# GpSimd's wait for a place in the ring of gathered rows: VectorE's add in place of TensorE's sum

## The chip, the cores and the metric

The kernel runs on one core of a Trainium2 chip. The metric is the device time of one execution in microseconds (us); the kernel before takes 2083.07 us, the median of 3 runs. Engines are named as in the profile: PE is TensorE's matmuls, PEld its weight loads, DVE VectorE, ACT ScalarE, POOL GpSimd, SP SyncE.

## What is computed

A network of four layers over 3125 nodes with 256 features and 50000 edges, all in float32. Layers one and three are graph layers, layers two and four mixtures of experts. The change touches only the sums over edges in the two graph layers. Cut to that, the reference is

```python
# layer 1: edges carry 64 features, dst is sorted
sender_features = nodes[senders]
msg_in = jnp.concatenate([sender_features, edges], axis=-1)
messages = msg_in @ W_message
agg = jax.ops.segment_sum(messages, receivers, num_segments=total_nodes)
...
# layer 3: h_sparse keeps the 32 largest of each row of feat @ W_neigh
msg = h_sparse[src]
summed = jax.ops.segment_sum(msg, dst, num_segments=n)
neigh = summed / jnp.maximum(deg, 1.0)[:, None]
return h_self + neigh
```

The kernel sums the gathered rows first and multiplies the sums by the weights afterwards.

## The kernel before

The nodes are 25 tiles of 128 rows. The edges, sorted by target, are cut into 98 groups of 512 (`NG` = 98), each of four columns of 128 edges (`GC` = 4). A group's targets lie within a window of 128 nodes. `sums_and_nodes` is called twice, with the tag O0 for layer 1 (rows from `n_rows`, with edge features) and with O1 for layer 3 (rows from `sparse_rows`, without). It runs the class `Sums` for the groups, last group first, and beside it the work on each node tile as soon as its sums are complete: `NodeMlp` in O0, a layer norm, three matrix layers and another norm; `NeighbourMeans` in O1, much shorter.

One group, number `o` in the order of work, passes through four engines:

- GpSimd, `gather`: four indirect DMAs (line 743), each of which fetches 128 rows of 1 KB, by the edges' source numbers, into place `o % 8` of the ring `G` (`GR` = 8 places). From the ninth group on it first waits for a place (the line that the change touches, 741).
- VectorE, `hot` (line 767): the one-hot matrix `OH` of the group's targets, in a ring of four.
- TensorE, `products` (line 758): the sum. It multiplies rows by `OH` into one of two PSUM banks: 8 matrix products of 128x128 in O1 (16 records in the profile), 12 in O0 (24 records), where 4 of them read the edge features `EA`. It waits for `OH`, the gathered rows and VectorE's add of group `o - 2`, which frees the bank, and its last product increments `summed`.
- VectorE, `add` (line 779): after writing the `OH` of group `o + 2` it waits for `summed`, adds the bank to the window of the table `sumT`, and increments `added`.

TensorE and VectorE take the groups at fixed points among their other work on node tiles (`group(0)` to `group(3)` in the methods `pe` and `dve`), 3 or 4 groups in each step; each engine runs its list in order, so an add stands behind whatever VectorE has before it. GpSimd does nothing else in these two stretches than the 392 indirect DMAs, in order. The edge features come by SyncE's DMAs, which wait for the sum of group `o - 4` and are not touched. ScalarE's copy of finished sums waits for `added`. The stages before, between and after (normalising, routing, experts, the product with both weight matrices) are separated by barriers of all engines, so a stretch that ends later moves everything behind it.

Of the kernel before, what the change touches and what calls it, by code (L numbers as in the profile page):

```python
# [19 lines left out]
GR = 8  # L20
# [6 lines left out]
def build(nc, a, out):  # L27
# [52 lines left out]
    with ExitStack() as ctx:  # L80
# [632 lines left out]
        class Sums:  # L713
# [24 lines left out]
            def gather(self, pool, o):  # L738
                g, s = NG - 1 - o, o % GR
                if o >= GR:  # L740
                    pool.wait_ge(self.summed, o + 1 - GR)
                for k in range(GC):
                    pool.indirect_dma_start(out=self.G[:, s, k, :], out_offset=None, in_=self.rows_dram,  # L743
                                            in_offset=bass.IndirectOffsetOnAxis(ap=src_tab[:, g, k:k + 1], axis=0)
                                            ).then_inc(self.gathered[s], 16)
# [1166 lines left out]
```

## Time and profile before

| what | value |
|---|---|
| median of 3 runs | 2083.07 us (2081.49 to 2083.76) |
| the profiled execution | 2088.08 us, its span 2086.3 us |
| PE busy | 1273.2 us (61%) |
| DVE busy | 758.2 us (36%) |
| ACT busy | 388.7 us (19%) |
| POOL busy | 1094.5 us (52%) |
| O0, from the first gather to the last | from 56.2 to 667.6 us |
| O1, from the first gather to the last | from 1234.5 to 1801.2 us |

The page gives each engine's busy time over the whole span, and the costliest groups of instructions with the idle time ahead of them and who ended it. The two lines on `L743 POOL DMA_INDIRECT` stand at its head: 392 gathers of 985 ns in O0 and 392 of 961 ns in O1. An idle time that is put down to "issue" is one in which the profile saw nothing waited for; "remote" is a wait that ended on a semaphore whose increment the profile can't give to an instruction that ended just then. TensorE's records carry a measured start and a modelled end.

### The profile page before, as it was taken

The page shows a single profiled execution, that of the slowest core. Times are in us where ns is not written, and L with a number is a line of the kernel's source. Part 1 is how long each engine was busy: PE and PEld are TensorE (multiplying, and loading weights), DVE is VectorE, ACT ScalarE, POOL GpSimd, SP SyncE. Part 2 cuts the span into 40 slices and gives each one's busy share as a digit, 9 for nine tenths or more (in the row PEclk, how much of TensorE's full clock was granted, in tenths as well). Part 3 has the DMA queues.
Part 4 walks back from the last instruction along what each step waited for, and adds up shares of the span by engine and source line. Part 5 has one row for each costly group of instructions (what it writes and reads, how often), then busy time and mean ns, then how long its engine had stood idle before and what let it go on. Part 6 is the DMA issues. An engine that isn't in the chain of part 4 may idle for free. (4 is left out here: it accounts for less than half of the span.)

```text
span 2086.3 us, 29303 instructions
## 1 busy us (share of the span) xinstructions
PE 1273.2 (61%) x7947; PEld 1132.2 (54%) x7948; DVE 758.2 (36%) x2256; ACT 388.7 (19%) x1296; POOL 1094.5 (52%) x1166
## 2 busy tenths in 40 slices
PE   0267877777788727999936533446454554539920
PEld 0256777767677626999812213445454544528920
DVE  5022444444444451111159951222222222364433
ACT  0000111111111102444334410000000000005533
POOL 2656656556665003222187736666666666315455
PEclk9778888889898759999956656677666766769965
DMA  5334434434433008999822233333333333203445
GB/s 175 103 101 113 111 102 109 108 102 115 109 107 106 18 5 302 351 353 348 294 78 81 78 125 95 91 94 100 98 97 98 99 96 99 62 32 107 130 127 156
DMA packets 204046, 264.53 MB, mean 127 GB/s; under 512 B 75150, under 2 KB 155040, under 8 KB 203670
## 3 DMA queue, kind: packets, MB, share of 16 engines
q0 software_dynamic: 48192, 131.35, 22.2%
q1 hardware_dynamic: 152882, 129.47, 18.9%
q10 hardware_dynamic: 2852, 2.24, 0.4%
q8 instruction: 58, 0.95, 0.2%
q14 instruction: 62, 0.51, 0.1%
HBM read 231.24 MB, written 32.04 MB: 126 GB/s over the span
## 5 line engine op out<-in xcount | busy, mean ns | idle before, releaser
L743 POOL DMA_INDIRECT O0G<-n_rows,src_tab x392 | 386.0, 985 | 267.0 <-issue 144.7
L743 POOL DMA_INDIRECT O1G<-sparse_rows,src_tab x392 | 376.8, 961 | 200.6 <-issue 121.3
L758 PE MATMUL O1ps_sums<-O1OH,O1G 128*128 128x128 f32 x1568 | 262.2, 338 | 158.9 <-DVE sumT L779 80.1
L758 PEld LDWEIGHTS O1ps_sums<-O1OH,O1G 128*128 128x128 f32 x1568 | 249.2, 250 | 166.8 <-issue 166.6
L758 PE MATMUL O0ps_sums<-O0OH,O0G 128*128 128x128 f32 x1568 | 227.2, 298 | 63.4 <-issue 49.7
L758 PEld LDWEIGHTS O0ps_sums<-O0OH,O0G 128*128 128x128 f32 x1568 | 212.3, 212 | 71.3 <-issue 71.0
L779 DVE TENSOR_TENSOR sumT<-sumT,O1ps_sums 128x256 f32 x98 | 41.2, 421 | 441.4 <-remote 340.4
L779 DVE TENSOR_TENSOR sumT<-sumT,O0ps_sums 128x384 f32 x98 | 54.3, 554 | 334.2 <-remote 191.9
L1363 POOL DMA_INDIRECT e0xs<-token_rows,e0idx x64 | 60.5, 945 | 204.7 <-ACT e0idx L1432 202.9
L758 PE MATMUL O0ps_sums<-O0OH,O0EA 128*128 128x128 f32 x784 | 115.9, 289 | 21.6 <-issue 21.2
L1389 PE MATMUL e0ps_h<-e0xT,e0W 128*128 128x128 f32 x1024 | 126.1, 277 | 1.5 <-DMA e0W<-in_L_ffn_w 1.5
L1644 PE MATMUL m0ps_d<-w_dense,m0nT 128*128 128x512 f32 x100 | 85.7, 1008 | 61.9 <-ACT m0nT L1617 61.9
L1389 PEld LDWEIGHTS e0ps_h<-e0xT,e0W 128*128 128x128 f32 x1024 | 120.7, 194 | 1.8 <-DMA e0W<-in_L_ffn_w 1.7
L1403 PE MATMUL e0ps_y<-e0W,e0hidT 128*128 128x256 f32 x512 | 120.9, 379 | 0.0
L758 PEld LDWEIGHTS O0ps_sums<-O0OH,O0EA 128*128 128x128 f32 x784 | 105.3, 205 | 21.2 <-issue 20.9
L1484 DVE TENSOR_TENSOR e0ys<-e0ps_y,e0b_rows 128x256 f32<-128x256 f32 x64 | 27.2, 425 | 226.2 <-PE e0ps_y L1403 226.2
L1763 PE MATMUL O1ps_g<-gate_w,O1nT 128*128 128x8 f32 x100 | 22.7, 337 | 141.8 <-ACT O1nT L1742 118.3
L962 PE MATMUL O0ps<-O0hT,w_mlp 128*128 128x128 f32 x600 | 96.8, 309 | 18.1 <-issue 10.5
L1363 POOL DMA_INDIRECT e1xs<-token_rows,e1idx x56 | 55.5, 992 | 91.4 <-ACT e1idx L1432 56.5
L1763 PEld LDWEIGHTS O1ps_g<-gate_w,O1nT 128*128 128x128 f32 x100 | 20.8, 291 | 149.0 <-ACT O1nT L1742 124.9
L962 PEld LDWEIGHTS O0ps<-O0hT,w_mlp 128*128 128x128 f32 x600 | 89.0, 224 | 20.1 <-issue 11.1
L1403 PEld LDWEIGHTS e0ps_y<-e0W,e0hidT 128*128 128x128 f32 x512 | 92.5, 190 | 9.9
(298 smaller groups left out, 2012.6 us busy)
## 6 DMA issues: line engine op xcount, KB each, us to landing
e0W<-in_L_ffn_w SPq DMA_DIRECT2D x128, 512.0 KB
O0EA<-in_edge_attr SPq DMA_DIRECT2D x97, 128.0 KB
expert_out<-e0ys SPq DMA_DIRECT2D x64, 128.0 KB
expert_out<-e1ys SPq DMA_DIRECT2D x56, 128.0 KB
O0G<-n_rows,src_tab POOLq DMA_INDIRECT x392
O1G<-sparse_rows,src_tab POOLq DMA_INDIRECT x392
e1W_all<-in_L_ffn_w SPq DMA_DIRECT2D x16, 256.0 KB
n_rows<-NR SPq DMA_DIRECT2D x5, 640.0 KB
```

Source lines behind the costliest of these rows:

```text
L743: pool.indirect_dma_start(out=self.G[:, s, k, :], out_offset=None, in_=self.rows_dram, in_offset=bass.IndirectOffsetOnAxis(ap=src_tab[:, g ...
L758: last = nc.tensor.matmul(self.ps[o % 2][:, half * P:(half + 1) * P], rows, self.OH[:, h, k, :], start=(k == 0), stop=(k == GC - 1))
L779: nc.vector.tensor_tensor(window, window, self.ps[o % 2][:, 0:self.halves * P].rearrange("p (h w) -> p h w", h=self.halves), ALU.add).then ...
L962: last = nc.tensor.matmul(ps_l[:, m * P:(m + 1) * P], w_mlp[:, l, k, m * P:(m + 1) * P], hT[:, s, k, :], start=(k == 0), stop=(k == K2 - 1))
L1363: pool.indirect_dma_start(out=xs[:, s, :], out_offset=None, in_=token_dram, in_offset=bass.IndirectOffsetOnAxis(ap=idx[:, s:s + 1], axis=0 ...
L1389: last = nc.tensor.matmul(ps_h[:, s % 2, j * P:(j + 1) * P], W1[:, s, k, j * P:(j + 1) * P], xT[:, s, k, :], start=(k == 0), stop=(k == K2 ...
L1403: last = nc.tensor.matmul(ps_y[:, s % 2, 0:D], hidT[:, s, j, :], rows, start=(j == 0), stop=(j == FJ - 1))
L1484: nc.vector.tensor_tensor(ys[:, s, :], ps_y[:, s % 2, 0:D], tile_of(b2_rows, e), ALU.add).then_inc(y_ready, 1)
L1644: last = nc.tensor.matmul(ps_d[:], nT[:, s, k, :], w_dense[:, k, :], start=(k == 0), stop=(k == K2 - 1))
L1763: last = nc.tensor.matmul(self.ps_g[:, 0:E1], self.nT[:, k, :], gate_w1[:, k, :], start=(k == 0), stop=(k == K2 - 1))
```

## The change

GpSimd's wait for a free place in the ring is moved from TensorE's semaphore to VectorE's. Both count groups, and the count waited for stays the same. One line changes; it is used in both stretches, 90 times in each. No instruction is added or removed.

```diff
             def gather(self, pool, o):
                 g, s = NG - 1 - o, o % GR
                 if o >= GR:
-                    pool.wait_ge(self.summed, o + 1 - GR)
+                    pool.wait_ge(self.added, o + 1 - GR)
                 for k in range(GC):
                     pool.indirect_dma_start(out=self.G[:, s, k, :], out_offset=None, in_=self.rows_dram,
```

## Rows read from the trace of the kernel before

**Rows 1.** Windows: both stretches while GpSimd gathers, and O1's end after it.

```profile
core 0: us, PE busy (x) PEld busy (x) DVE busy (x) ACT busy (x) POOL busy (x), PEclk, DMA share, GB/s
56.00:668.00 612.00, 443.76 (x3069) 415.98 (x3069) 231.49 (x651) 78.04 (x241) 386.02 (x392) 0.84 0.40 109
...
1234.00:1802.00 568.00, 276.22 (x1662) 264.32 (x1662) 125.25 (x323) 21.64 (x67) 376.83 (x392) 0.69 0.36 103
1802.00:1815.00 13.00, 10.75 (x92) 10.32 (x92) 5.22 (x13) 1.49 (x4) 0.00 (x0) 1.00 0.06 20
```

**Rows 2.** Waits of POOL: us in total, times, longest us.

```profile
POOL O0G L743 <- remote: 79.3, 39, 6.5
POOL O1G L743 <- remote: 71.7, 27, 6.1
...
POOL O0G L743 <- PE O0ps_sums L758: 43.0, 14, 4.1
...
POOL O1G L743 <- PE O1ps_sums L758: 7.6, 6, 2.5
```

**Rows 3.** Timeline of POOL, O1: start us, us; in brackets idle before, releaser.

```profile
1558.04 0.94 POOL L743 DMA_INDIRECT O1G<-sparse_rows,src_tab  x1 [2.34 <-remote]
...
1575.43 0.94 POOL L743 DMA_INDIRECT O1G<-sparse_rows,src_tab  x1 [2.72 <-remote]
...
1589.34 0.95 POOL L743 DMA_INDIRECT O1G<-sparse_rows,src_tab  x1 [0.30 <-issue]
1592.90 0.94 POOL L743 DMA_INDIRECT O1G<-sparse_rows,src_tab  x1 [2.61 <-remote]
```

**Rows 4.** Timeline of DVE, the adds of the same stretch.

```profile
1563.21 0.42 DVE L779 TENSOR_TENSOR sumT<-sumT,O1ps_sums 128x256 f32 x1 [3.19 <-issue]
...
1581.35 0.42 DVE L779 TENSOR_TENSOR sumT<-sumT,O1ps_sums 128x256 f32 x1 [3.38 <-PE O1ps_sums L758]
...
1592.77 0.42 DVE L779 TENSOR_TENSOR sumT<-sumT,O1ps_sums 128x256 f32 x1 [9.73 <-remote]
```

**Rows 5.** Timeline of POOL, two restarts in O0.

```profile
285.11 1.03 POOL L743 DMA_INDIRECT O0G<-n_rows,src_tab  x1 [2.17 <-remote]
...
293.65 0.94 POOL L743 DMA_INDIRECT O0G<-n_rows,src_tab  x1 [3.74 <-PE O0ps_sums L758]
```

**Rows 6.** Timeline of DVE, the adds at these restarts.

```profile
286.50 0.55 DVE L779 TENSOR_TENSOR sumT<-sumT,O0ps_sums 128x384 f32 x1
...
293.52 0.56 DVE L779 TENSOR_TENSOR sumT<-sumT,O0ps_sums 128x384 f32 x1 [5.87 <-PE O0ps_sums L758]
```

**Rows 7.** Waits of PE: the only one on O0's gathered rows.

```profile
PE O0ps_sums L758 <- DMA O0G<-n_rows,src_tab: 12.6, 1, 12.6
```

**Rows 8.** Timeline of PE, O0, while GpSimd fills the ring.

```profile
73.93 1.13 PE L758 MATMUL O0ps_sums<-O0OH,O0G 128*128 128x128 f32 x8 [2.12 <-issue]
...
87.10 0.37 PE L758 MATMUL O0ps_sums<-O0OH,O0G 128*128 128x128 f32 x1 [2.43 <-issue]
```

**Rows 9.** Timeline of POOL, the first pause of each stretch.

```profile
108.41 0.94 POOL L743 DMA_INDIRECT O0G<-n_rows,src_tab  x1 [6.49 <-remote]
...
1285.58 0.94 POOL L743 DMA_INDIRECT O1G<-sparse_rows,src_tab  x1 [6.09 <-remote]
```

**Rows 10.** Timeline of PE, O1: the first two sums, and sums about the restarts.

```profile
1246.88 6.72 PE L758 MATMUL O1ps_sums<-O1OH,O1G 128*128 128x128 f32 x32 [24.62 <-issue]
...
1559.67 1.64 PE L758 MATMUL O1ps_sums<-O1OH,O1G 128*128 128x128 f32 x11
...
1580.53 2.02 PE L758 MATMUL O1ps_sums<-O1OH,O1G 128*128 128x128 f32 x16
```

**Rows 11.** Timeline of DVE, O1: the second add, and the first and last of the last five.

```profile
1285.45 0.42 DVE L779 TENSOR_TENSOR sumT<-sumT,O1ps_sums 128x256 f32 x1 [28.47 <-remote]
...
1805.41 0.42 DVE L779 TENSOR_TENSOR sumT<-sumT,O1ps_sums 128x256 f32 x1 [1.79 <-PE O1ps_sums L758]
...
1813.22 0.42 DVE L779 TENSOR_TENSOR sumT<-sumT,O1ps_sums 128x256 f32 x1 [1.81 <-PE O1ps_sums L758]
```

## The prediction

> **What bounds the kernel now.** I read the windows first. The gathers of O0 and O1 take 612 and 568 us, 57% of the span, and in neither is an engine busy throughout: of O0's 612 us PE has 444 and POOL 386, of O1's 568 us PE has 276 and POOL 377 [rows 1]. Next the timeline of POOL: a gather is 0.95 us with 0.30 us to the next [rows 3], so a group of four takes 5.0 us and 98 groups 490 us. What O0 and O1 last beyond 490 us, GpSimd stands still. The table of waits says on what: in O0 53 pauses with 122.3 us (79.3 + 43.0, 39 + 14), in O1 33 with 79.3 us (71.7 + 7.6, 27 + 6) [rows 2]. These contain each the usual 0.30 us. They are the waits of line 741: the ring is full, and GpSimd goes on 0.13 us after an add begins (1575.43, 1592.90 against 1592.77; 293.65 against 293.52) [rows 3 to 6], because both wait for the same sum. TensorE in turn hardly waits for rows: the table has one such wait in O0, 12.6 us at its start [rows 7].
>
> So GpSimd waits for TensorE, TensorE not for GpSimd's rows, and one would call TensorE the bound. The rows don't bear that out in O1. Its last five adds, after the last gather, begin 7.81 us from first to last, 1.95 us a group [rows 11]; while gathers run a group takes 568/98 = 5.8 us. TensorE is slow only beside GpSimd. The start of the stretches shows it directly. In O0, PE does 8 products in 1.13 us from 73.93 us on, and then one in 2.8 us (0.37 and 2.43 idle, put down to nothing) [rows 8]; that ends when GpSimd has filled the ring and paused for 6.49 us [rows 9]. In O1 the products of the first two groups are on record from 1246.88 to 1253.60 [rows 10], yet the second add begins at 1285.45 with VectorE idle for 28.47 us before it [rows 11], 6 us after GpSimd's first run of gathers ended (1285.58 less 6.09) [rows 9]. In the middle of O1: GpSimd restarts at 1575.43; a sum arrives at 1581.35, 5.9 us later; the next one's products are on record from 1580.53 to 1582.55 [rows 10], but its add begins at 1592.77 [rows 4], 2.5 us after GpSimd paused again at 1590.29 [rows 3]. I conclude that in a run of gathers sums get through for some 6 us, then they are held until about 2 us after the next pause. What holds them (the products, their write to PSUM or the semaphore) the profile doesn't say; it shows only the moments.
>
> **The change.** One edit, one answer to work out: when GpSimd goes on, and what that costs. No instruction is added, and queued behind the wait are only the four gathers of the group and all later ones; the edge features' DMAs are in SyncE's queue and keep their own wait.
>
> The delay of one restart. Now GpSimd starts 0.13 us after the add's start, then 0.13 us after its end, as far as another semaphore takes as long. In O1 an add is 0.42 us [rows 4]: 33 x 0.42 = 14 us. In O0 it is 0.55 us, but VectorE may be at other work. At 285.11 GpSimd goes on with the sum, and the add begins at 286.50 [rows 5, 6]: the restart would move to 286.50 + 0.55 + 0.13 = 287.18, by 2.07 us. Nine of the 53 pauses look so, the others like the one at 293.65, by 0.56 us: 44 x 0.55 + 9 x 2.1 = 43 us, 0.81 us each. Waits that don't stop GpSimd now may stop it for a few tenths; I leave them at nothing, the add of eight groups back is long done there. Delays in sum: 57 us.
>
> What reaches the end. If rows were what TensorE waits for, or GpSimd the bound, all 57 us; if TensorE were the bound on its own, none. Neither fits what I read. In the pattern above a pause costs l, in which GpSimd does nothing, and buys a window w after the restart, in which sums get through. The sums of a stretch need a fixed total of such windows. A later restart adds e to both: TensorE works on in e. So the number of pauses falls by w/(w + e), each costs l + e, and all pauses together change by (l + e)/l x w/(w + e). From the rows l is 79.3/33 = 2.40 us in O1 and 122.3/53 = 2.31 us in O0, and e is 0.42 and 0.81 us. For w the upper end is 6 us (the sum at 5.9 us came in time, the next did not). The lower end is 3 us: after the restart at 1558.04 products that end on record at 1561.31 [rows 10] have their add at 1563.21 [rows 4], 1.9 us later instead of 0.1, so lateness has set in some 3 us after the restart.
> - w = 6: O1 1.175 x 0.935 = 1.098, +7.8 us; O0 1.351 x 0.881 = 1.190, +23.2 us; sum +31 us.
> - w = 3: O1 1.175 x 0.877 = 1.031, +2.4 us; O0 1.351 x 0.787 = 1.064, +7.8 us; sum +10 us.
> I take the middle, w = 4.5: O1 +5.9 us, O0 +17.7 us, sum +23.6 us, since either end is one pair of rows. Nothing behind gives it back, because a barrier follows each stretch. The profiled execution, 2088.1 us (its span 2086.3), would take about 2112 us; against the median it is 2083.1 + 23.6 = 2106.7, and I forecast 2106 us. A difference of 4 us (0.2%) is about what a measurement can tell from none.
>
> **Rivals.**
>
> First, the ring hides it (2083 us, 2080 to 2087). When GpSimd waits, up to eight groups are gathered ahead of TensorE, and 7 groups of 5.8 us are 40 us of stock against a delay of at most 2.1 us. For it: only one wait for rows in O0 [rows 7]. If TensorE's slowness had a cause of its own, the restart's moment wouldn't matter. Against it: the last adds at 1.95 us and the two starts, where the hold ends with GpSimd's pause [rows 8 to 11]. The Trainium skill speaks for this rival: its page "SBUF — State Buffer", section "SBUF: two separate sides", says that only the ports which GpSimd and VectorE share cause contention, and that TensorE never waits on anyone. By that rule the sum would be nothing. The trace doesn't agree as I read it, with one product in 2.8 us beside gathers. The page "DMA: Bandwidth & Descriptors", section "Anatomy of one DMA", gives some 2.0 us fixed and 436 GB/s, from which I estimate 2.3 us for a gather of 128 KB; by that too rows would lie ready long before use.
>
> Second, the whole delay (2125 to 2140 us). GpSimd does nothing useful in its pauses, so 490 us plus pauses is the length, and if TensorE can use none of the longer pause, because its next product stands behind VectorE's or ScalarE's work on tiles, all 57 us come: 2140. For it: PE's own waits for ScalarE in O1 are of that kind. Against: in O0 PE is busy 73% of the time [rows 1], so it has work queued.
>
> Third, faster (2060 to 2079 us). O0 has 90 groups that wait and 53 pauses, 1.7 groups a run, so some 35 runs of two. A run of two groups is 10 us, and sums are held from about 6 us after the restart to 12 us, 2 us after the pause began; a run of one group is 5 us and holds nothing. If the wait for adds, which come less evenly than sums, splits runs of two, TensorE wins each time up to those 6 us; I take half, 3 us, as products begun go on meanwhile. Then 8 runs split would cancel the 23.6 us, and 14 would give 2065 us. It decides where two adds follow each other by more than 5.0 us. For it: adds like the one at 286.50 are 1.5 us later than their sum. Against it: such an add pushes the wait for itself and not that for the next, so as many runs should be joined as split.
>
> **How the numbers follow.** Forecast, part of the delay arrives (2090 to 2125 us): 0.60. The ring hides it: 0.17. The whole delay: 0.06. Faster: 0.17. That the wait doesn't do as it says I leave out: the same count on a semaphore that lags by one add can't let GpSimd go earlier. Within 0.2% fall the hidden case, 0.02 of the faster and 0.01 of the forecast's lower edge: same 0.20, slower 0.65, faster 0.15. For 8 in 10 the range goes from 2076 us (which leaves out 0.13, most of the faster case) to 2128 us (which holds w = 6 at 2114 us and twice its distance from the forecast, and leaves out 0.07, the whole delay and a little).
>
> **What would show it.** In the profile of the changed kernel every restart of GpSimd after a pause should come 0.13 us after the end of an add, not its start. Pauses should be fewer or as many, and longer: in O1 about 33 with 85 us, in O0 about 50 with 140 us. PE's busy time should stay. O0 should be longer by about 18 us from first gather to last add and O1 by 6 us, and all other stages as long as before. The forecast is wrong in its core if the pauses' total grows by under 4 us (the ring hides it) or falls (the third rival), and in its size if PE's holds begin at another time after a restart than before.

## The result, and the profile after

The change makes the kernel slower: 2111.05 us, the median of 4 runs (2104.76 to 2115.39), against 2083.41 us for the kernel before (4 runs, 2081.49 to 2086.55). The ratio is 1.0121, with a 95% interval of 1.0099 to 1.0143. The forecast was 2106 us.

The profiled execution of after took 2115.39 us, its span 2113.5 us, 27.2 us more than the span of before. Where they are is seen from the line of all gathers and the line of all adds (in each: shortest, median and longest ns, then the start of the first and of the last). Before, by line 743 and by the tile `sumT`:

```profile
L743 POOL DMA_INDIRECT O0G<-n_rows,src_tab x392: 940/946/2028, 56.2 to 666.7; - x196
L743 POOL DMA_INDIRECT O1G<-sparse_rows,src_tab x392: 940/946/1467, 1234.5 to 1800.3; - x196
```

```profile
L779 DVE TENSOR_TENSOR sumT<-sumT,O0ps_sums x98: 541/555/558, 72.3 to 694.5; 128x384 f32 x98
L779 DVE TENSOR_TENSOR sumT<-sumT,O1ps_sums x98: 414/422/424, 1256.0 to 1813.2; 128x256 f32 x98
```

After:

```profile
L743 POOL DMA_INDIRECT O0G<-n_rows,src_tab x392: 943/949/2028, 57.0 to 692.3; - x196
L743 POOL DMA_INDIRECT O1G<-sparse_rows,src_tab x392: 943/949/1386, 1251.4 to 1821.1; - x196
```

```profile
L779 DVE TENSOR_TENSOR sumT<-sumT,O0ps_sums x98: 539/555/558, 72.4 to 714.1; 128x384 f32 x98
L779 DVE TENSOR_TENSOR sumT<-sumT,O1ps_sums x98: 414/422/424, 1272.8 to 1840.5; 128x256 f32 x98
```

From the first gather to the last add O0 goes from 638.3 to 657.1 us (+18.8) and O1 from 578.7 to 589.1 us (+10.4). That is 29.2 us, and all other stages together are 2 us shorter, as the prediction had it. In O0 the gathers themselves take longer, 635.3 us for 610.5 (+24.8), and the rest after the last gather is 6.0 us shorter (21.8 for 27.8). In O1 it is the other way: the gathers take 569.7 for 565.8 us (+3.9), and the rest after them 19.4 for 12.9 us (+6.5). These splits compare one execution with one other. Executions of the changed kernel on a single chip differ by up to 19 us (the third chip, below), so a few us in a part of a stretch carry little.

The waits of GpSimd in the trace after (us in total, times, longest us), which answer to [rows 2]:

```profile
POOL O0G L743 <- DVE sumT L779: 146.3, 57, 6.7
...
POOL O1G L743 <- DVE sumT L779: 78.3, 25, 6.4
```

O0 has 57 waits with 146.3 us for 53 with 122.3, O1 has 25 with 78.3 for 33 with 79.3. So O0 has more and longer pauses (2.57 us for 2.31 each), O1 fewer and longer ones (3.13 for 2.40) with nearly the same sum. Together they grew by 23.0 us. The prediction had said that it would be wrong in its core if they grew by under 4 us. Counted instead as idle times over 0.4 us in the timeline of POOL, whatever the profile puts them down to, O0 goes from 51 with 121.5 us to 61 with 151.9, and O1 from 31 with 80.2 to 22 with 79.9; the expectations of some experiments use this count.

A restart in O1 of after, in the timeline of POOL, and the add that released it in that of DVE (start us, us; in brackets idle before, releaser):

```profile
1332.10 1.15 POOL L743 DMA_INDIRECT O1G<-sparse_rows,src_tab  x1 [4.19 <-DVE sumT L779]
```

```profile
1331.41 0.42 DVE L779 TENSOR_TENSOR sumT<-sumT,O1ps_sums 128x256 f32 x1 [15.88 <-remote]
```

The add ends at 1331.83 and GpSimd goes on at 1332.10, 0.27 us later. Before, it went on 0.13 us after an add's start [rows 3, 4]. In O1 a restart is thus 0.56 us later against the same add (0.42 + 0.27 - 0.13), where the prediction had 0.42. All 83 restarts after an idle time over 0.4 us in this trace (61 in O0, 22 in O1) come 0.26 to 0.28 us after the end of an add. Counted in the same way over the trace of before, restarts moved to 0.27 us after the end of their adds would be 0.97 us later on average in O0 and 0.56 in O1, 49 and 17 us in sum. In O0, the same two timelines of after:

```profile
293.19 1.15 POOL L743 DMA_INDIRECT O0G<-n_rows,src_tab  x1 [4.39 <-DVE sumT L779]
...
301.13 0.95 POOL L743 DMA_INDIRECT O0G<-n_rows,src_tab  x1 [3.02 <-DVE sumT L779]
...
306.39 0.95 POOL L743 DMA_INDIRECT O0G<-n_rows,src_tab  x1 [0.55 <-DVE sumT L779]
```

```profile
300.30 0.56 DVE L779 TENSOR_TENSOR sumT<-sumT,O0ps_sums 128x384 f32 x1 [6.78 <-PE O0ps_sums L758]
...
305.56 0.56 DVE L779 TENSOR_TENSOR sumT<-sumT,O0ps_sums 128x384 f32 x1 [2.09 <-PE O0ps_sums L758]
```

Here too it is 0.27 us (300.86 to 301.13, 306.12 to 306.39). The last row is something that before doesn't have: a group that would have followed without a pause waits 0.55 us instead of the usual 0.30, because adds 5.26 us apart are wider apart than the 5.0 us of a group. Counting the groups between idle times over 0.4 us in the timeline of POOL, O0 has 16 runs of one group and 32 of two before, and 39 of one and 17 of two after. Idle times under 1.1 us are 13 after and none before, those over 2.6 us 29 after and 13 before.

PE's busy time, which the prediction expected to stay, is 1286.2 us for 1273.2, 1% more.

### The profile page after: what moved, and what is told of

It is laid out like the page before. It is cut to its first block and busy times, and to the rows that moved or that the text cites. A ratio compares the mean times of both kernels' runs of the same rounds, so it can differ in the third digit from the quotient of the medians.

```text
span 2113.5 us, 29303 instructions
## 1 busy us (share of the span) xinstructions
PE 1286.2 (61%) x7947; PEld 1136.9 (54%) x7948; DVE 759.7 (36%) x2256; ACT 388.8 (18%) x1296; POOL 1094.2 (52%) x1166
## 5 line engine op out<-in xcount | busy, mean ns | idle before, releaser
L758 PEld LDWEIGHTS O0ps_sums<-O0OH,O0G 128*128 128x128 f32 x1568 | 216.6, 217 | 54.4 <-issue 54.0
L1363 POOL DMA_INDIRECT e0xs<-token_rows,e0idx x64 | 60.7, 948 | 204.6 <-ACT e0idx L1432 202.8
L962 PE MATMUL O0ps<-O0hT,w_mlp 128*128 128x128 f32 x600 | 99.9, 311 | 25.7 <-issue 18.8
L1484 DVE TENSOR_TENSOR e0ys<-e0ps_y,e0b_rows 128x256 f32<-128x256 f32 x64 | 27.2, 425 | 226.3 <-PE e0ps_y L1403 226.3
L1446 ACT ACTIVATE e0hidT<-e0ps_h,b_cols 128x128 f32<-128x128 f32 x256 | 73.3, 368 | 92.4 <-issue 53.3
L923 ACT ACTIVATE O0yT<-O0ps,b_mlp 128x128 f32<-128x128 f32 x100 | 31.3, 364 | 305.3 <-remote 222.8
```

The costliest lines, as they stand in the source:

```text
L758: last = nc.tensor.matmul(self.ps[o % 2][:, half * P:(half + 1) * P], rows, self.OH[:, h, k, :], start=(k == 0), stop=(k == GC - 1))
L923: last = nc.scalar.activation(yT[:, m, :], ps_l[:, m * P:(m + 1) * P], ACT.Relu, bias=b_mlp[:, l, m:m + 1])
L962: last = nc.tensor.matmul(ps_l[:, m * P:(m + 1) * P], w_mlp[:, l, k, m * P:(m + 1) * P], hT[:, s, k, :], start=(k == 0), stop=(k == K2 - 1))
L1363: pool.indirect_dma_start(out=xs[:, s, :], out_offset=None, in_=token_dram, in_offset=bass.IndirectOffsetOnAxis(ap=idx[:, s:s + 1], axis=0 ...
L1446: last = nc.scalar.activation(hidT[:, s, j, :], ps_h[:, s % 2, j * P:(j + 1) * P], func, bias=b1_cols[:, ds(e * FJ + j, 1)])
L1484: nc.vector.tensor_tensor(ys[:, s, :], ps_y[:, s % 2, 0:D], tile_of(b2_rows, e), ALU.add).then_inc(y_ready, 1)
```

## The experiments

They ran on four other chips, here called the second to the fifth, each beside runs of the kernel before on the same chip. That turned out to matter more than any edit. The kernel before takes 2083 us on the first chip, 1879 on the second, 2068 on the third, 2063 on the fourth and 1877 on the fifth. Every comparison below is within one chip.

### Second chip: the wait in O0 alone, a ring of five, a pause for every group

```diff
-                    pool.wait_ge(self.summed, o + 1 - GR)
+                    pool.wait_ge(self.added if self.with_edges else self.summed, o + 1 - GR)
```

> GpSimd waits for VectorE's add in O0 alone; in O1 it waits for the sum as before. Theory H (sums are held while GpSimd gathers without a pause, so that part of each restart's delay arrives): O0 takes 18 us more from first gather to last add, O1 as before, in all 2101 us (2094 to 2108). Rival W (a restart's whole delay arrives in O0, the 43 us worked out for it, and something in O1 gives 15 us back): 2126 us. Rival E (equal shares, the cost goes by waits and not by an add's length or lateness): 2097 us.

Measured: 1878.73 us (10 runs) against 1878.95 us (19 runs), ratio 0.9996, 0.9982 to 1.0010. All three forecasts in it start from 2083 us, and the base itself is 204 us lower here. The costliest groups of this run's trace (busy us, mean ns | idle before, by releaser) say why:

```profile
L743 POOL DMA_INDIRECT O0G<-n_rows,src_tab x392 | 385.1, 982 | 162.1 <-issue 159.7 <-DVE sumT L779 2.4
L743 POOL DMA_INDIRECT O1G<-sparse_rows,src_tab x392 | 380.0, 969 | 133.1 <-issue 129.1 <-PE O1ps_sums L758 4.0
...
L779 DVE TENSOR_TENSOR sumT<-sumT,O0ps_sums 128x384 f32 x98 | 54.3, 554 | 242.2 <-PE O0ps_sums L758 242.2
L779 DVE TENSOR_TENSOR sumT<-sumT,O1ps_sums 128x256 f32 x98 | 41.4, 422 | 371.4 <-PE O1ps_sums L758 371.4
```

GpSimd never pauses for a place: its wait for the add has 2.4 us in all, in 8 waits of the usual 0.30 us, and the 392 gathers of a phase follow each other in 504 us (O0) and 499 us (O1). VectorE's adds wait only until a product of TensorE ends. None of the adds' waits is "remote", where before on the first chip has 191.9 and 340.4 us of these. Such waits, with adds up to 32 us after the last record of their products (1253.60 and 1285.45) [rows 10, 11], are what I called held sums, and this chip has none. The 204 us between the chips are about the 201.6 us of pauses in [rows 2] (122.3 + 79.3). So on this chip the ring is never full, and where GpSimd's wait never ends last, the change's half in O0 costs nothing. In O0 it is TensorE that waits for rows here, 92.3 us in all, where it had 12.6 us on the first chip [rows 7]:

```profile
L758 PE MATMUL O1ps_sums<-O1OH,O1G 128*128 128x128 f32 x1568 | 278.1, 351 | 215.2 <-issue 138.7 <-DVE O1OH L767 47.8 <-DMA O1G<-sparse_rows,src_tab 28.7
...
L758 PE MATMUL O0ps_sums<-O0OH,O0G 128*128 128x128 f32 x1568 | 210.3, 291 | 97.6 <-DMA O0G<-n_rows,src_tab 92.3 <-DVE O0OH L767 3.4 <-DVE sumT L779 1.4
```

The same rows speak against an obvious rival, that TensorE merely calculates faster on this chip. Its products of gathered rows take 351 ns on average in O1 and 291 ns in O0; on the first chip they take 338 and 298 ns. In O1 they are slower here and still no sum is late.

```diff
-                if o >= GR:
-                    pool.wait_ge(self.summed, o + 1 - GR)
+                if o >= 5:
+                    pool.wait_ge(self.summed, o + 1 - 5)
```

> GpSimd waits for TensorE's sum as before, but uses the ring as if it had 5 places: each restart waits for the sum three groups later, some 17 us. Theory H: TensorE still has five groups of stock, the number of windows it needs is the same, so the stretches take as long as before; the first run of gathers is 6 groups long in place of 9, and the long hold that follows it shorter, so 2066 to 2085 us. Rival W (each later restart moves what follows by its delay): the change delayed a restart by 0.4 to 0.8 us and cost 27.6 us; a delay of 17 us, even if only the 86 first ones of it count once, gives over 2180 us. Rival B (TensorE is bound by itself, and the ring hides GpSimd): 2083 us, with the first hold as long as before.

Measured: 1876.49 us (10 runs) against 1878.95, ratio 0.9988, 0.9972 to 1.0005, for the same reason. Neither of these two runs tells the theories apart; they show only that five places are enough where no sum is late.

```diff
+                pool.wait_ge(self.idled, o) if o else None
+                nc.gpsimd.memset(self.idle[:], 0.0).then_inc(self.idled, 1)
```

These lines stand at the end of `gather`, with a tile `idle` of 128x1024.

> As before, and after each group of four gathers GpSimd sets 1024 columns of a scratch tile to zero (some 0.95 us), and waits for the one before: a group takes it some 6.3 us and no run of gathers is longer than 5 us. Theory H: no run is long enough to hold sums, if a gap of over 1 us ends a run. The pauses for a place in the ring nearly go (under 10 in each stretch after the first), an add follows its last product by 0.1 to 0.2 us, and the stretches last 98 x 6.3 = 617 us and a tail: O0 some 15 us shorter, O1 some 40 us longer, in all 2095 to 2120 us. Rival B (TensorE's slowness is its own): adds come late by 5 to 11 us in O1 as before, and the ring pauses stay, 10 us less in sum than the 1.25 us a group that GpSimd takes longer.

Measured: 2033.73 us (1 run), 155 us more. In the timeline of POOL the memset is 0.96 us, and a group takes 5.83 us (1356.49 to 1362.32) instead of 5.0:

```profile
1356.49 0.95 POOL L745 DMA_INDIRECT O1G<-sparse_rows,src_tab  x1 [0.17 <-issue]
...
1361.19 0.96 POOL L749 MEMSET O1idle<- 128x1024 f32 x1
1362.32 0.95 POOL L745 DMA_INDIRECT O1G<-sparse_rows,src_tab  x1 [0.17 <-issue]
```

196 groups x 0.83 us are 163 us, nearly all of which arrive (155). On such a chip GpSimd's own gathers set the length of both phases, and nearly each us that they are delayed is a us of the kernel's time. There were no held sums on which the pause could have worked, so the question that this run was made for is not answered by it, and the edit was not timed on a chip with pauses.

### Third chip: the changed kernel again, and two places with either wait

The changed kernel itself, timed again:

> The changed kernel itself, timed against the kernel before on whatever chip this call gets. What is at stake: on the second chip the kernel before takes 1879 us instead of 2083, and GpSimd's 392 gathers of each phase run without a single pause (added in O0 alone, and a ring of 5, both gave 1879 +- 3 there). Theory 'pauses': the move only costs where GpSimd waits for a place at all; if the kernel before takes about 1879 us here, the changed one is within 0.2% of it (1875 to 1883), its trace without pauses; if the kernel before takes about 2083 us here, the changed one takes 2105 to 2117. Rival 'own price': the wait for VectorE's add costs something by itself in each of 196 groups, whatever the chip: over 0.4% slower (1887 us or more) on the faster chip too.

Measured: 2093.65 us (6 runs) against 2068.03 us (11 runs), ratio 1.0116, 1.0084 to 1.0147. The chip is one with pauses, and the ratio is that of the first chip within the error. O0 has 47 waits with 125.3 us for the add, O1 24 with 68.0. From the first gather to the last add O0 takes 642.0 us and O1 584.6. The kernel before has no trace on this chip; on the fourth, where it is 5 us faster, these are 616.9 and 576.0 us (below).

```diff
-                if o >= GR:
-                    pool.wait_ge(self.summed, o + 1 - GR)
+                if o >= 2:
+                    pool.wait_ge(self.summed, o + 1 - 2)
```

> GpSimd waits for TensorE's sum of the group two before, so the ring of 8 is used as 2 places; all else as before. Worked out from the traces of the second chip: from a group's first gather to the end of its last 4.7 us, rows there 1.8 us later, the sum 2.9 us in O0 (0.25 us after the rows) and 2.0 to 3.8 us in O1, 0.1 us to the restart. So two groups in turn take 9.7 us in O0 and 8.6 to 10.4 us in O1, against the 10.0 us that GpSimd needs for them. Theory 'plain chain' (no sums that come late): +0 to +15 us over the kernel before. Theory 'hold' (sums come late while GpSimd gathers, as in the first chip's traces, and are let go about 2 us after it pauses): 12 to 12.5 us for two groups, 590 to 610 us for each phase, so 2090 to 2150 us on a chip where the kernel before takes 2083. What a late sum costs with no place to spare is in this run.

Measured: 2048.81 us (4 runs), ratio 0.9897, 0.9866 to 0.9927, so 19 us faster than before. Neither theory had a gain: "hold" had 7 to 67 us more than before, so it is wrong by 26 us or more, and "plain chain" has its sign wrong.

The next has the same edit with `self.added` for `self.summed`:

> As the run with two places, but GpSimd waits for VectorE's add of the group two before: the change on record made where each wait ends last. The add ends 0.70 us (O0, 384 columns) and 0.56 us (O1, 256 columns) after the sum in the second chip's traces. Theory 'whole' (each restart later by all of the add): against the run with two places +0.35 us a group in O0 and +0.28 in O1, less what GpSimd's own 5.0 us a group hide of it (0.15 in O0, nothing to 0.28 in O1): +20 us in O0 and +15 to +25 in O1, +35 to +45 us in all. Theory 'hold' with its release by the pause: the later restart lets more sums through, +15 to +30 us. Rival 'hidden': the add's time is made up elsewhere, under +10 us.

Measured: 2101.75 us (4 runs), ratio to before 1.0153, 1.0122 to 1.0184, and 52.9 us over the run with two places and the wait for the sum. That is above all three ranges. The lines of the gathers and of the adds with the wait for the sum (a fence for each view):

```profile
L743 POOL DMA_INDIRECT O0G<-n_rows,src_tab x392: 940/946/2034, 57.5 to 657.6; - x196
L743 POOL DMA_INDIRECT O1G<-sparse_rows,src_tab x392: 940/946/1453, 1205.1 to 1773.4; - x196
```

```profile
L779 DVE TENSOR_TENSOR sumT<-sumT,O0ps_sums x98: 542/554/557, 70.7 to 665.2; 128x384 f32 x98
L779 DVE TENSOR_TENSOR sumT<-sumT,O1ps_sums x98: 420/422/424, 1222.5 to 1780.1; 128x256 f32 x98
```

and with the wait for the add:

```profile
L743 POOL DMA_INDIRECT O0G<-n_rows,src_tab x392: 940/947/2034, 56.5 to 700.6; - x196
L743 POOL DMA_INDIRECT O1G<-sparse_rows,src_tab x392: 940/947/1422, 1244.8 to 1822.6; - x196
```

```profile
L779 DVE TENSOR_TENSOR sumT<-sumT,O0ps_sums x98: 541/555/557, 69.5 to 706.8; 128x384 f32 x98
L779 DVE TENSOR_TENSOR sumT<-sumT,O1ps_sums x98: 420/422/424, 1261.2 to 1829.3; 128x256 f32 x98
```

The gathers of O0 go from 600.1 to 644.1 us (+44.0), those of O1 from 568.3 to 577.8 us (+9.5). The delay weighs 4.6 times as much in O0 as in O1; with eight places the gathers have +24.8 against +3.9. No give-back is seen in O0 with two places. In the run with the wait for the sum, 60 restarts follow an idle time over 0.4 us, and if each came 0.27 us after the end of its add they would be 43 us later in sum: 44.0 arrive. In O1 there are 60 too, with 33 us in sum, and 9.5 arrive.

### Fourth chip: O1 alone, three places, the kernel before, and O1 without GpSimd

The kernel before, unedited, for its trace on this chip:

> The kernel before, unedited, for its trace on the same chip as the others of this call. If it takes over 2060 us here: GpSimd's pauses 110 to 130 us in O0 and 72 to 85 us in O1, with adds up to 20 us behind the products. If it takes about 1879 us: no pause, every add 0.14 us after the last product of its group but for some in O0.

Measured: 2065.13 us in this one run; the median of before on this chip is 2063.45 us (15 runs). Its gathers and adds:

```profile
L743 POOL DMA_INDIRECT O0G<-n_rows,src_tab x392: 940/946/2027, 57.7 to 649.4; - x196
L743 POOL DMA_INDIRECT O1G<-sparse_rows,src_tab x392: 940/946/1442, 1213.0 to 1772.0; - x196
```

```profile
L779 DVE TENSOR_TENSOR sumT<-sumT,O0ps_sums x98: 539/554/557, 74.4 to 674.6; 128x384 f32 x98
L779 DVE TENSOR_TENSOR sumT<-sumT,O1ps_sums x98: 410/421/424, 1234.2 to 1789.0; 128x256 f32 x98
```

Its pauses are 102.5 us in O0 (51) and 67.3 us in O1 (29), somewhat fewer than expected: the faster a chip runs this kernel, the fewer us of pauses its trace has (201.6 at 2083 us, 169.8 at 2063 us, none in the runs on the chip with 1879 us).

```diff
-                    pool.wait_ge(self.summed, o + 1 - GR)
+                    pool.wait_ge(self.summed if self.with_edges else self.added, o + 1 - GR)
```

> GpSimd waits for VectorE's add in O1 alone; O0 is as before. On a chip whose traces have GpSimd's pauses (the kernel before over 2060 us): the forecast had +5.9 us for O1 of +23.6; the two traces of the first chip have +10.4 us from the first gather of O1 to its last add, with the pauses' sum unchanged (80.2 and 79.9 us, 31 and 22 of them). So +4 to +11 us here, ratio 1.002 to 1.005, and pauses of 76 to 84 us in O1. Rival 'half': each phase bears half of the change's 25 us (+12 us or more, 1.006 and over). Rival 'all in O0': within 0.1%. On a chip without pauses (the kernel before about 1879 us): no difference.

Measured: 2076.51 us (10 runs) against 2063.45, ratio 1.0058, 1.0031 to 1.0084. The median says +13 us, the interval +6 to +17, so it takes in much of what I expected and the rival "half"; only "all in O0" is out. The profiled execution was one of the shortest of its kernel (span 2062.3 us), and its O1 takes 579.0 us from the first gather to the last add (rows below), 3.0 us more than the 576.0 us of the unedited kernel: the gathers are 8.8 us longer (567.8 for 559.0) and the rest after them 5.8 us shorter (11.2 for 17.0). How much of the change's 1.2% is O1's stays open between these.

```profile
L743 POOL DMA_INDIRECT O1G<-sparse_rows,src_tab x392: 940/946/1496, 1213.7 to 1781.5; - x196
```

```profile
L779 DVE TENSOR_TENSOR sumT<-sumT,O1ps_sums x98: 412/421/424, 1233.6 to 1792.7; 128x256 f32 x98
```

```diff
-                if o >= GR:
-                    pool.wait_ge(self.summed, o + 1 - GR)
+                if o >= 3:
+                    pool.wait_ge(self.summed, o + 1 - 3)
```

> GpSimd waits for TensorE's sum of the group three before; all else as before. With two places the pauses' sum was 203 us (112.9 in O0, 90.1 in O1) against 202 us (121.7 and 80.2) with eight in the first chip's trace, and what was gained was the end: the last add of O0 came 7.3 us after the last gather instead of 27.5. Theory 'rate' (TensorE's sums get through only so many per us beside gathers, and the places only say when GpSimd learns of it): three places give 200 to 210 us of pauses again and an end of about 10 us, so 15 to 22 us less than before, ratio 0.989 to 0.993. Rival 'short runs' (two places gain since GpSimd's runs are short, and three let late sums pile up again): 0.995 or more. On a chip without pauses: within 0.2% of before, as with five places.

Measured: 2043.55 us (4 runs) against 2063.45, ratio 0.9899, 0.9860 to 0.9938, which is "rate". Its gathers and adds:

```profile
L743 POOL DMA_INDIRECT O0G<-n_rows,src_tab x392: 940/947/2033, 57.0 to 651.7; - x196
L743 POOL DMA_INDIRECT O1G<-sparse_rows,src_tab x392: 940/947/1457, 1198.7 to 1760.1; - x196
```

```profile
L779 DVE TENSOR_TENSOR sumT<-sumT,O0ps_sums x98: 542/555/558, 71.5 to 659.8; 128x384 f32 x98
L779 DVE TENSOR_TENSOR sumT<-sumT,O1ps_sums x98: 411/422/424, 1215.8 to 1766.8; 128x256 f32 x98
```

With three places for eight the gathers take 594.7 for 591.7 us in O0 and 561.4 for 559.0 in O1, so nearly the same. The last add comes 8.1 for 25.2 us after the last gather in O0 and 6.7 for 17.0 in O1, 27.4 us less in sum. Together -22.0 us, and the medians have -19.9. The pauses are 109.3 + 75.7 = 185 us for 169.8; the 200 to 210 that I had expected were the first chip's. So from three places up the number hardly changes how fast groups pass; it sets how many groups are left for TensorE when GpSimd is done, and with eight these are done with GpSimd idle. This version beats both kernels on a chip with pauses. It wasn't timed on one without; five places made no difference there.

Last, O1's rows by SyncE. The edit sends O1's fetches from SyncE's queue as plain copies of whole blocks of 128 consecutive rows, into the same ring behind the same wait. It leaves out the choice of rows by the edges' source numbers, so O1 sums other rows than the reference; only its time is of use:

```diff
+                    if not self.with_edges:
+                        row = (o * GC + k) % (T - 1) * P
+                        pool.dma_start(self.G[:, s, k, :], self.rows_dram[row:row + P, :]).then_inc(self.gathered[s], 16)
+                        continue
...
-                        for o in range(NG):
+                        for o in range(NG if with_edges else 0):
                             sums.gather(pool, o)
...
-                            if with_edges:
-                                for o in groups_of(u):
-                                    sums.load_edges(sp, o)
+                            for o in groups_of(u):
+                                if with_edges:
+                                    sums.load_edges(sp, o)
+                                else:
+                                    sums.gather(sp, o)
```

> O1's rows are fetched by SyncE as plain copies of whole blocks (not the rows of the index list, so the sums of O1 are of other rows), and GpSimd does nothing in O1; O0 is as before. It took 1599.6 us on the chip without pauses. On a chip with pauses: theory 'beside gathers' (TensorE's sums are signalled late only while GpSimd gathers): no late adds in O1, its pauses gone, those of O0 left: 1600 + 122 + 20 = 1740 us, 1715 to 1765. Rival 'the chip' (signals of TensorE are late there whatever fetches the rows): adds up to 10 us and more behind their products in O1 as well, 1790 us and over.

Measured: 1709.66 us (1 run), 5 us below the range of "beside gathers" and far from the rival's 1790 us. The same kernel on the second chip:

> O1's rows are not gathered: SyncE copies 128 consecutive rows of sparse_rows into each place, 4 copies a group and the same bytes, in the order and with the wait on sums of GpSimd's gathers, so the sums in O1 are of other rows than the reference's; GpSimd has nothing to do in O1. Theory H, by GpSimd's work: no sum is held, an add follows its last product by 0.1 to 0.2 us, and a group takes TensorE 2 to 3.5 us: O1 lasts 200 to 340 us in place of 579 us, in all 1710 to 1850 us. Theory H2 (the rows' traffic into SBUF holds the sums, whoever starts it): sums come late as before and O1 takes over 450 us. Rival B (TensorE's own pace): O1 570 to 580 us, in all 2083 us.

took 1599.59 us (1 run). Its three forecasts start from 2083 us; against before on that chip the run is 279 us shorter, where "theory H, by GpSimd's work" had 233 to 373 us less and its rivals less or nothing. The two lines of the adds on the fourth chip, by costliest groups:

```profile
L783 DVE TENSOR_TENSOR sumT<-sumT,O0ps_sums 128x384 f32 x98 | 54.2, 553 | 334.2 <-remote 169.6 <-PE O0ps_sums L762 164.4
L783 DVE TENSOR_TENSOR sumT<-sumT,O1ps_sums 128x256 f32 x98 | 41.3, 422 | 95.1 <-PE O1ps_sums L762 95.0
```

O0, with GpSimd's gathers, has 169.6 us of "remote" waits; O1, without them, has none in the same execution. O1's adds by the tile `sumT` take 208 us from first to last, where those of the unedited kernel take 555:

```profile
L783 DVE TENSOR_TENSOR sumT<-sumT,O1ps_sums x98: 420/422/425, 1227.4 to 1435.4; 128x256 f32 x98
```

That stretch by window (columns as in [rows 1]):

```profile
1226.00:1437.00 211.00, 201.77 (x1745) 196.54 (x1743) 129.66 (x332) 23.33 (x71) 0.00 (x0) 1.00 0.83 251
```

PE is busy for 202 of 211 us beside 251 GB/s of transfers, where O1 of before has 276 of 568 us beside 103 GB/s [rows 1]. On the second chip O1's adds take 208.7 us from first to last with this edit, so without gathers the two chips no longer differ in O1. So it isn't the bytes that make the sums late; it goes with what the edit takes away. The edit takes three things away at once, GpSimd's work, the indirect form and the scattered rows, so which of them does it isn't shown.

### Fifth chip: O0 alone once more

I wanted the wait for the add in O0 alone on a chip with pauses. The edit is that of the first experiment.

> GpSimd waits for VectorE's add in O0 alone; O1 is as before. It cost nothing on the chip without pauses. On a chip with pauses (the kernel before over 2060 us) the forecast had +17.7 us for O0; the two traces of the first chip have +18.7 us from the first gather of O0 to its last add, with 30 us more of pauses and 6 us less after the last gather; and the whole change less the change in O1 alone, by their ratios on two chips (1.0116 less 1.0058), would leave +12 us. So +12 to +20 us, ratio 1.006 to 1.010, and 110 to 150 us of pauses in O0 in 50 to 61 of them. Rival 'whole delay' (every restart later by the add with none of it given back): 50 restarts x 0.7 us or more, +35 us, 1.016 and over. Rival 'given back' (the longer pause lets out sums that would have needed it later): within 0.2%.

Measured: 1878.04 us (12 runs) against 1876.51 us (17 runs), ratio 1.0010, 0.9998 to 1.0021. This was a chip without pauses again (in its trace the waits for the add have 1.5 us in all), so the run repeats the second chip's and says nothing on the split. The whole change was not run on such a chip; only its half in O0 was, twice. O0 alone on a chip with pauses was not measured.

## Why the prediction was right, and where it was not

**What bounds the kernel: right on the chips with pauses, and incomplete.** GpSimd stands still because sums come late, and they come late beside its own gathers: O1 without gathers shows it on the fourth chip. But gathers alone don't do it. On the second and fifth chips GpSimd gathers without a break for 500 us a phase, and every sum is on time. So "sums get through for some 6 us, then they are held" is no property of the kernel; it is at most what happens beside these gathers on three of the five chips. What differs between the chips I can't say, and that the change was timed on a chip with pauses was luck: on the second or the fifth, where its O0 half cost nothing, the forecast would most likely have failed with the same working.

**That a pause ends 0.13 us after the end of the add: wrong by 0.14 us.** It is 0.27 us. The 0.13 us after an add's start that I took over was the gap between two engines that wait for the same sum, and not the time from an instruction's end to the start of the one that waits for it. The delay e was thus 0.56 us in O1 and about 0.95 in O0, not 0.42 and 0.81; by my own formula with w = 4.5 that gives 7.7 + 20.2 = 27.9 us where I had 23.6. Measured are 27.6 us in the medians. That they meet is not a proof of the formula, as the next paragraph shows. The nine restarts with a late VectorE belong to that one execution, too: the trace of before on the fourth chip has one of 50.

**That part of the delay arrives: right as a total, not in its parts.** The working says that pauses become a little fewer in both phases and that each grows by e. In O1 there are 25 for 33, and each grew by 0.73 us; their sum fell by 1.0 us instead of rising by 5.9. The cost of O1 came mostly by another way, the 6.5 us more after the last gather. It may be nothing but where the last run of gathers happens to end: with the same wait in O1 on the fourth chip it went the other way, 5.8 us less after the last gather and 8.8 us more before it. In O0 I had 50 pauses with 140 us, and there are 57 with 146.3. The sizes are +18.8 for +17.7 us in O0, which is close, and +10.4 for +5.9 in O1, which is not; and a formula whose count goes the wrong way in one phase, and whose sum does in the other, is not confirmed by them. The total owes part of its closeness to luck.

**What stands in place of the formula.** Three and eight places give the same length of all gathers within 3 us on the fourth chip, and two places on the third are within 10 us of these, so TensorE's sums get through at some rate that these moves of the pauses hardly change. It would fit that most of a delay in O1 is given back (of some 17 us with eight places the gathers show +3.9 and, on the fourth chip, +8.8; of 33 us with two, +9.5). It doesn't fit O0. There about half arrives with eight places (+24.8 of some 50 us) and all with two (+44.0 of 43). That VectorE's adds come in between longer work on node tiles there, more than 5.0 us apart, so that runs of two groups break up (39 runs of one for 16), may be the reason, and is argued, not shown. Why a part arrives, and which part, stays open.

**The first rival, the ring hides it,** is what two of five chips do, though not for its reason. It spoke of a full ring as stock ahead of TensorE; there the ring is never full, and the change is free because the wait never ends last. On the chips with pauses it fails. The Trainium skill's rule on the page "SBUF — State Buffer", section "SBUF: two separate sides", that TensorE never waits on anyone, agrees with the traces of the second and fifth chips and with O1 by SyncE, where no sum is late. It doesn't account for those of the other three, where TensorE's sums come late while GpSimd gathers. Whether anything waits for a port of SBUF there no run shows, so they don't contradict the rule either.

**The second rival, the whole delay,** had 57 us for a delay of 0.66 us a pause on average. 29.2 us arrived in the two stretches of the traces and 27.6 in the medians, and with e as measured the whole would be 67 us. With two places, and so with little in stock, 52.9 us arrived of 76: all of it in O0, and under a third in O1.

**The third rival, splitting runs of two,** decides where adds are more than 5.0 us apart. They are, and the splits came, 15 runs of two fewer, more than the 14 from which I had a gain of 18 us. No gain came. Its price was wrong: I took it that a run of one group holds nothing. In O0 of after, pauses behind a single group can be long (3.02 us at 301.13, 4.39 at 293.19), so lateness is not reset by a short break. The trace of before has it already: in its O0 the 16 pauses behind one group average 2.76 us and the 31 behind two 2.01 us.

## What to carry to other kernels

To free a buffer from the engine that reads it last, not from the one after, is right even with eight places, wherever the trace shows the producer waiting for places. Ask first whether it waits at all: if no wait on that line ends last, the choice costs nothing, and the same kernel can be in the one case on one chip and in the other on the next. A deep ring doesn't add speed when its consumer is the slower one; it only leaves more to be done after the producer has finished, and here three places gained 1.0% over eight, on the one chip, with pauses, where that was timed. How late a sum is can itself depend on the chip, so time a change on more than one before a cause is named.

## What the runs showed that I had not expected

- One kernel, five chips: 2083, 1879, 2068, 2063 and 1877 us, the runs of one chip within about 1% of each other. Nearly all of the difference is in the two stretches with gathers (202.8 of the 206.8 us between the traces of the first and second chips), and in these in GpSimd's pauses.
- On a chip with pauses TensorE's records run on while the signal of a finished sum is up to 32 us late [rows 10, 11], and it is on time once SyncE fetches O1's rows (98 adds in 208 us beside 251 GB/s). At the start of O0 it is the products themselves that come slowly, one in 2.8 us [rows 8]. The Trainium skill's page "Perfetto Trace Analysis", section "Tensor Engine Instruction (MATMUL, LD_WEIGHTS)", says that TensorE's end times are computed and that the acknowledgement of PSUM and the semaphore's way come after them; so a late acknowledgement would not show in its records. No run here shows whether the products, the acknowledgement or the semaphore is late.
- A GpSimd instruction that waits for VectorE's instruction starts 0.27 us after its end (1331.83 to 1332.10, 300.86 to 301.13), and 0.13 us after the start of VectorE's where both waited for the same sum (1592.77 to 1592.90 [rows 3, 4]).
